# Row numbers of the scatter: a place for each of the 23 tiles in place of four shared ones

## What is computed

```python
normed = hidden_states * rsqrt(var + 1e-08) * norm_weight
shared = maximum(normed @ sw1 + sb1, 0.0) @ sw2 + sb2
probs = sigmoid(flat @ router_w.T)
scores, idx = top_k(probs, TOPK)                 # TOPK = 2, E = 8
w = scores / (sum(scores) + 1e-06)
comb = zeros((T, E)).at[arange(T)[:, None], idx].add(w)
h = maximum(einsum('td,edh->teh', flat, ew1) + eb1, 0.0)     # hidden 512
eo = einsum('teh,eho->teo', h, ew2) + eb2
out = shared + einsum('teo,te->to', eo, comb)
```

## Time and profile before

| | |
|---|---|
| median of 3 runs | 1669.17 us |
| the profiled execution's own time | 1669.32 us |
| its span in the profile | 1667.0 us, 36532 instructions |
| PE busy | 1377.0 us, 83% |
| DVE busy | 1096.7 us, 66% |
| ACT busy | 942.1 us, 57% |
| POOL busy | 602.0 us, 36% |
| DMA | 108.50 MB, mean 65 GB/s |

### The profile page before, as it was taken

How to read it: one execution, slowest core, us unless ns; L and a number is a source line. 1 busy time by engine, 2 the same in 40 slices (tenths; PEclk the granted TensorE clock), 3 DMA queues, 4 the chain that set the end, 5 groups by cost and what they waited for, 6 DMA issues and landing times. The chain is left out here.

```text
span 1667.0 us, 36532 instructions
## 1 busy us (share of the span) xinstructions
PE 1377.0 (83%) x13193; PEld 1123.7 (67%) x13193; DVE 1096.7 (66%) x2274; ACT 942.1 (57%) x1676; POOL 602.0 (36%) x664
## 2 busy tenths in 40 slices
PE   4888885799999999759999999999982775877880
PEld 4777773587777787548888888888881663655550
DVE  5888885667777667547667667676666763645552
ACT  4778785665665665445555555555542553655550
POOL 2322220355555556533122122122110763255552
PEclk9999997799999999969999999999995777999995
DMA  4222221322212222130000000000002211145535
GB/s 142 82 96 80 92 89 56 120 81 71 67 49 76 83 70 79 26 97 2 14 14 2 14 15 2 14 15 2 1 2 63 83 50 47 49 137 159 163 130 169
DMA packets 91916, 108.50 MB, mean 65 GB/s; under 512 B 19327, under 2 KB 56703, under 8 KB 91779
## 3 DMA queue, kind: packets, MB, share of 16 engines
q1 hardware_dynamic: 82466, 80.68, 16.2%
q0 software_dynamic: 9312, 26.03, 4.5%
HBM read 61.06 MB, written 29.82 MB: 55 GB/s over the span
## 5 line engine op out<-in xcount | busy, mean ns | idle before, releaser
L827 POOL TENSOR_TENSOR b_h_lo<-b_h,b_h_hi 128x512 fp32r<-128x512 f32 x168 | 216.5, 1293 | 179.0 <-ACT b_h_hi L851 178.5
L1227 POOL TENSOR_TENSOR c_prob<-c_prob,c_recip 128x520 f32<-128x520 f32 x64 | 67.9, 1067 | 401.8 <-DVE c_recip L1517 401.8
L846 ACT ACTIVATE b_zg<-b_zg 128x512 f32<-128x512 f32 x168 | 97.6, 581 | 81.6 <-PE b_zg L890 81.4
L851 ACT ACTIVATE b_h_hi<-b_h 128x512 fp32r<-128x512 f32 x168 | 105.1, 626 | 65.7 <-DVE b_h L1055 65.6
L1907 POOL DMA_INDIRECT planes_dram<-d_y_out,d_back x92 | 93.7, 1019 | 123.3 <-DVE d_y_out L2215 101.4
L1055 DVE TENSOR_TENSOR b_h<-b_zg,b_uw 128x512 f32<-128x512 f32 x168 | 116.2, 691 | 32.0 <-ACT b_zg L846 26.7
L1048 DVE TENSOR_TENSOR b_uw<-b_zu,b_gw 128x512 f32<-128x512 f32 x128 | 88.2, 689 | 57.3 <-PE b_zu L890 50.9
L2184 DVE TENSOR_TENSOR d_h_lo<-d_h,d_h_hi 128x512 fp32r<-128x512 f32 x124 | 81.4, 685 | 29.1 <-ACT d_h_hi L1945 19.2
L1945 ACT ACTIVATE d_h_hi<-d_h 128x512 fp32r<-128x512 f32 x124 | 77.3, 624 | 40.1 <-DVE d_h L2178 40.0
L1270 ACT ACTIVATE c_probT<-c_s 128x1024 f32<-128x1024 f32 x64 | 65.6, 1025 | 51.0 <-PE c_s L1417 50.6
L328 POOL TENSOR_TENSOR a_qx<-a_qT,headmask 128x256 f32<-128x256 f32 x64 | 37.9, 613 | 147.2 <-ACT a_qT L363 147.2
(11 more groups left out here) (357 smaller groups left out, 4248.8 us busy)
## 6 DMA issues: line engine op xcount, KB each, us to landing
rows_dram<-a_blank SPq DMA_DIRECT2D x32, 520.0 KB, 3.2
b_gw<-gates_dram SPq DMA_DIRECT2D x64, 256.0 KB, 3.9
d_up_slot<-d_up_tab POOLq DMA_DIRECT2D x15, 512.0 KB, 3.0
d_down_slot<-d_down_tab POOLq DMA_DIRECT2D x15, 512.0 KB
d_xg<-rows_dram SPq DMA_DIRECT2D x23, 260.0 KB
b_gm<-gates_dram SPq DMA_DIRECT2D x32, 160.0 KB, 3.9
c_craw<-in_c_ctxT_dram SPq DMA_DIRECT2D x8, 512.0 KB, 4.0
d_pay<-planes_dram SPq DMA_DIRECT2D x16, 256.0 KB, 4.5
```

What stands on the lines that cost most here:

```text
L827: pool.tensor_tensor(h_lo[:, m % HS, :], h[:, m % HF, :], h_hi[:, m % HS, :].bitcast(F32), ALU.subtract).then_inc(lo_done.sem, 1)
L846: act.activation(zg_ps[:, n % ZG, :], zg_ps[:, n % ZG, :], ACT.Silu).then_inc(sg_done.sem, 1)
L851: act.activation(h_hi[:, m % HS, :], h[:, m % HF, :], ACT.Copy).then_inc(hi_done.sem, 1)
```

## The change

`back` gets a place for each of the 23 tiles (TILES = 23) in place of four used in turn, and VectorE's wait for the scatter of tile t-4 before the tail of tile t is left out. `tail` and `pad` stay as they are, and so does the wait before y_out.

```diff
-        back = sb("back", [P, 4, GROUP], mybir.dt.int32)
+        back = sb("back", [P, TILES, GROUP], mybir.dt.int32)
...
-                            planes, bass.IndirectOffsetOnAxis(ap=back[:, t % 4, u:u + 1], axis=0),
+                            planes, bass.IndirectOffsetOnAxis(ap=back[:, t, u:u + 1], axis=0),
...
                     t = k + 1 - FIRST
-                    if t >= 4:
-                        dve.wait_ge(added[t % 2], 16 * GROUP * ((t - 4) // 2 + 1))
                     dve.wait_ge(xg_in[t % 2], 16 * (t // 2 + 1))
                     link(dve.tensor_copy(tail[:, t % 4, :, :], xg[:, t % 2, :, 0:2]), t_step)
...
-                    dve.scalar_tensor_tensor(out=back[:, t % 4, :], in0=pad[:, :], scalar=-1.0, in1=tail[:, t % 4, :, 0],
+                    dve.scalar_tensor_tensor(out=back[:, t, :], in0=pad[:, :], scalar=-1.0, in1=tail[:, t % 4, :, 0],
                                              op0=ALU.add, op1=ALU.add).then_inc(tail_done.sem, 1)
```

## The result

The changed kernel takes 1625.75 us in the median of four runs (1624.25 to 1629.37), the kernel before 1668.7 in four runs on the same chip. The ratio is 0.9747, 95% interval 0.9726 to 0.9768: 43 us faster, where 40 were forecast (1629, range 1625 to 1642). The profiled execution has a span of 1623.5 us against 1667.0.

A forecast was written before the change was run, and what follows sets the result against it. The loop from y_out through four scatters and their landing to VectorE's tail copy was taken as the bound. 1669.17 - 41.15 (19 steps cut to 7.30 us) = 1628.0, plus 1 us for joint load: 1629 us, range 1625 to 1642.

The forecast's parts named there:

- The loop as the bound: Tile part: y_out, four scatters, landing, tail copy, next y_out, 9.03 us a turn, sets the pace; no engine does.
- The rival that the wait only changes its name: VectorE at the tail copy really waits for xg or something else; time 1667 to 1671 us; chance 0.03.
- The step of 7.30 us as the next bound: TensorE's chain over ScalarE and VectorE, 6.74 us busy with a pause before the first z product, takes over.
- the unseen joint load of scatters, slot copies and xg: Added over the 15 steps with slots; bounds were nothing and 17 us, taken as 1 us.
- 41.15 us: Saving from tile 3 to tile 22, where 19 steps go from 179.85 us to 138.70 us.
- The cycle of 6.5 us: GpSimd's time per tile, from first scatter through the down_slot issue plus 0.3 us of waiting; 0.8 us below 7.30.
- The sign: In the tile steps GpSimd would wait 0.8 to 1.2 us per step for y_out if the forecast was right.
- that rival: GpSimd becomes the bound in the tile steps as more scatters meet VectorE's work: 1641 us, upper end 1664; chance 0.06.
- T + 6.9: When xg has come, T being the start of a tile's first z product; wanted at T + 8.8, 1.9 us left.
- the contention: Slot copies make xg late in the slot steps: steps of 7.6 to 8.4 us, 1632 to 1646 us; chance 0.15.
- The end: From y_out of tile 19 GpSimd issues 16 scatters without a break, about 1.3 us each; forecast as unchanged.
- the slower rival: Denser tile steps bring TensorE's 1.2 GHz level: steps of 11.0 us, +29 us, 1698 us; chance 0.02.

## Why the prediction was right

**The loop as the bound.** Right. Put back, the wait gives back the whole time; loaded with a memset, the loop grows nearly by the memset; moved behind y_out, or given one more place, the wait costs nothing. The rival that the wait only changes its name falls by the first and third of these.

**The step of 7.30 us as the next bound.** Right to 0.01 us. Tiles 1 to 3 of the kernel before ran without the wait, and the chain through x_hi that ended their pause is what the run with the early x_hi took away. I took 1 us for the unseen joint load of scatters, slot copies and xg; it was nothing between tile 3 and tile 22 (138.74 for 138.70). One reason given was not right: that 41.15 us is less than the 48.6 us waited because VectorE waits for x_hi in an undisturbed step anyway. It does so in the disturbed steps too: between tile 3 and tile 22 VectorE was idle ahead of x_lo for 37.4 us before and 33.9 after. What grew is its idle time ahead of h_lo, which waits for ScalarE's h_hi, from 0.6 to 10.5 us. The sum doesn't rest on this. The forecast of 1629 is 3 us above the median; the steps gave 41.1 of the 43 us, and the remaining 2 are within what executions differ by.

**GpSimd.** The cycle of 6.5 us is what its rows give in the changed kernel too: a usual wait of 1.12 us for y_out, of which 0.30 is the pause before any scatter, leaves 0.82 of slack, as forecast. But once GpSimd is late it needs only 6.22 us (1505.27 less 1497.66, less the memset), because the first scatter then takes 1.02 in place of 1.21 us, so the slack that a delay can use is 1.1 us. The sign was right. The rule of the Trainium skill (SBUF — State Buffer, "Who interferes with whom") that stood beside that rival hardly came to bear on the scatters: their mean went from 1.02 to 1.04 us and the longest from 1.42 to 1.50, and with the early x_hi, in denser steps, the mean is 1.02. It is more VectorE's copy that suffered. With the large memset behind the scatters, VectorE's and GpSimd's timelines have these rows:

```profile
1510.36 1.18 DVE L2224 COPY d_tail<-d_xg 128x8 f32<-128x8 f32 x1
...
1510.11 1.40 POOL L1912 MEMSET d_xn<- 128x1536 f32 x1
```

The copy of 8 columns, 0.17 us elsewhere, ended at 1511.54, with the memset's end at 1511.51. The same section of the Trainium skill says that copies can enter a mode that shares a port pair with GpSimd and that the later one blocks fully; this pair of rows agrees. Two other copies of that run took 1.77 and 1.80 us: each began 0.35 us before the memset, while the fourth scatter ran, and ended with the memset, and their steps took 8.11 and 8.14 us. In the changed kernel, where it meets only scatters, a copy took up to 0.40 us, and no step was longer for it.

**xg.** Predicted to have come at T + 6.9 and wanted at T + 8.8. In the step with T = 1488.66, xg was issued at 1493.51, 0.8 us later than worked out, its packets were through at about 1496.0 (T + 7.3), and TensorE turned it at 1497.46 (T + 8.8). The slack was 1.5 us, not 1.9. Of the 0.8 us, 0.55 lie between the first bias load and xg (3.34 us in place of 2.79), the rest came with the tail copy of 0.40 us ahead of h. The slot copies were through before xg began, so the contention did not come, and TensorE's turn waited for xg in none of the 19 steps.

**The end.** +0.36 us, forecast as unchanged. Right: GpSimd's 16 scatters in a row set it in both.

**The clock.** It rose from 0.95 to 1.00 over the whole stretch, against the slower rival.

## What to carry to other kernels

A wait's cost is found by following what is queued behind it back to what it waits for: if that closes a loop, the loop's length can be the step, and one more buffer, or the same wait placed behind the instruction that feeds the loop, can take it away; here both did. Steps of the same stage that happen to run without the wait, the first ones of a ring of buffers, show what comes next better than any sum. And a change that pays little under one bound (the early x_hi, 9 us, most of it from the long steps) can be worth twice that once the bound is gone (19 us), so the second candidate is worth measuring again.

## What the runs showed of the hardware that I had not expected

The long steps of the loop go together with instruction fetches at one moment. In the kernel before, five copies waited 3.2 to 4.7 us in place of 2.4, and each time one packet of the instruction queue began to move 0.9 to 1.3 us after the start of the tile's fourth scatter. For the wait of 4.70 us, the scatter started at 1496.00, the packet at 1497.1, and the copy went at 1500.52, 4.5 us after the scatter in place of 2.24. The window from 1497 to 1498 has this row of queues (kind, packets, MB, share of 16 engines):

```profile
q8 instruction: 1, 0.02, 9.5%
```

9.5% of 16 engines over 1 us is 1.5 us of one engine's time. In the run with the wait put back, all five long steps have such a packet 0.9 to 1.7 us after the fourth scatter. So it is 10 of 10 in the gap between the last scatter and its landing, when the copies of the slots come next, each with a landing 0.9 to 2.3 us late.

Elsewhere the packet went with little or nothing. It came between the scatters once in the kernel before (1438.6), and from 0.4 us before the fourth scatter to 0.05 us after it five times in the run with the early x_hi and the wait: no landing was more than 0.1 us late. It came 0.1 to 0.3 us before the fourth scatter five times in the kernel before with the memset: two landings were late, by 0.4 and 0.14 us, and these are its steps of 10.64 and 10.39 us.

That it is the scatter's share on the taken engine, or the slot copies overtaking it, was not tried, so the cause stays open. The five long steps held 8.5 us more than steps of 9.03 us in the profile of the kernel before. With the loop open no step of the changed kernel is longer than 7.31 us.
